# Causal attention scores on halves of the TensorE array, with the tokens of even sequences stored second half first

## What is computed

```
h      = x @ W.T + b + 2 * lora(x)                          # per sequence
q, k, v = dequant(h, 4-bit weights)                          # 32 query heads, 8 key/value heads, 128 wide
q, k   = rope(q), rope(k)                                    # tables by the token's place in its sequence
scores = q @ k.T / sqrt(128); scores = where(key <= query, scores, -max)
x      = x + dequant(softmax(scores) @ v, output weights)
x      = x + ffn(low_rank(x))                                # layer norm, two int8-like linears, gelu
```

## Time and profile before

| what | value |
|---|---|
| time, median of 3 runs (lowest to highest) | 568.68 us (568.56 to 568.96) |
| the profiled execution's own time | 569.7 us |
| its span, first to last instruction | 567.9 us |
| PE busy | 542.2 us, 95% |
| DVE busy | 485.0 us, 85% |
| POOL busy | 400.2 us, 70% |
| ACT busy | 363.0 us, 64% |
| granted TensorE clock, mean | 1.000 |

### The profile page before, as it was taken

How to read it: one execution, slowest core, us unless ns; L and a number is a source line. 1 busy time by engine, 2 the same in 40 slices (tenths; PEclk the granted TensorE clock), 3 DMA queues, 4 the chain that set the end, 5 groups by cost and what they waited for, 6 DMA issues and landing times.

```text
span 567.9 us, 10485 instructions
## 1 busy us (share of the span) xinstructions
PE 542.2 (95%) x3135; PEld 425.0 (75%) x3139; DVE 485.0 (85%) x626; ACT 363.0 (64%) x940; POOL 400.2 (70%) x410
## 2 busy tenths in 40 slices
PE   6999989999999999999999999999999999987885
PEld 3555768888888888888888888888888888865432
DVE  3553859997999799979997999799979998976897
ACT  3573567657665766576657665766576656665895
POOL 3005577799779977997799779977997799851063
PEclk9999999999999999999999999999999999999999
DMA  8752435422442244124512451245124312200003
GB/s 289 180 123 76 123 88 160 113 56 58 137 124 51 62 133 126 43 65 133 128 37 66 134 132 33 61 136 136 34 61 135 97 34 61 80 1 1 1 20 129
DMA packets 38172, 51.93 MB, mean 91 GB/s; under 512 B 12100, under 2 KB 20452, under 8 KB 38148
## 3 DMA queue, kind: packets, MB, share of 16 engines
q1 hardware_dynamic: 35652, 46.94, 31.3%
q10 hardware_dynamic: 2016, 3.48, 1.9%
q0 software_dynamic: 480, 1.22, 0.7%
HBM read 28.55 MB, written 2.10 MB: 54 GB/s over the span
## 4 chain that ended last, share of the span: by engine, by line
PE 80%; DVE 10%; issue 3%; DMA 2%; ACT 2%; POOL 2%; ACTq 0%; SPq 0%; DVEq 0%; POOLq 0%
PE pair L1378 23%; PE pair L1379 23%; PE flow L1367 9%; PE flow L1494 9%; PE flow L1486 4%; PE pair L1315 4%; DVE y_max L1191 2%; DVE raw_v L1081 1%; PE flow L1372 1%; DMA stage<-in_x 1%; PE flow L1315 1%; DMA swap_q<-raw_q 1%; DVE rope_c L1203 1%; DVE ctx_lo L1102 1%; DVE probs L1203 1%
## 5 line engine op out<-in xcount | busy, mean ns | idle before, releaser
L1095 DVE SCALAR_TENSOR_TENSOR accT<-pair,so_now,accT 128x1024 f32<-128x1024 f32 x125 | 157.2, 1274 | 14.8 <-PE pair L1379 13.9
L1081 DVE SCALAR_TENSOR_TENSOR raw_q<-pair,sc_now,raw_q 128x1024 f32<-128x1024 f32 x90 | 115.4, 1283 | 6.2 <-ACT raw_q L777 2.8
L560 POOL TENSOR_TENSOR probs<-probs,rowinv 128x512 f32<-128x512 f32 x64 | 66.8, 1044 | 65.4 <-DVE rowinv L1068 65.4
L722 ACT ACTIVATE probs<-flow,negmax 128x128 f32<-128x128 f32 x248 | 87.6, 369 | 32.8 <-DVE negmax L1049 32.8
L1378 PE MATMUL pair<-ctx_hi,wo 128*128 128x512 f32 x256 | 104.9, 410 | 2.8 <-issue 1.5
L1378 PE MATMUL pair<-h_hi,wq 128*128 128x512 f32 x240 | 100.0, 417 | 0.3 <-ACT raw_q L777 0.3
L1379 PE MATMUL pair<-ctx_lo,wo 128*128 128x512 f32 x256 | 100.2, 392 | 0.0
L1379 PE MATMUL pair<-h_lo,wq 128*128 128x512 f32 x240 | 94.1, 392 | 0.0
L529 POOL TENSOR_TENSOR rope_s<-swap_q,consts 128x512 f32<-128x512 f32 x62 | 80.2, 1293 | 9.2 <-DMA swap_q<-raw_q 9.2
L541 POOL TENSOR_TENSOR qT<-rope_c,rope_s 128x512 f32<-128x512 f32 x62 | 79.3, 1280 | 4.4
L529 POOL TENSOR_TENSOR rope_c<-raw_q,consts 128x512 f32<-128x512 f32 x62 | 78.8, 1293 | 0.0
(11 more groups left out here) (242 smaller groups left out, 966.3 us busy)
## 6 DMA issues: line engine op xcount, KB each, us to landing
swap_q<-raw_q SPq DMA_DIRECT2D x62, 256.0 KB, 3.7
wq_i<-in_L_attn_qw_q SPq DMA_DIRECT2D x8, 1024.0 KB, 5.6
wo_i<-in_L_attn_qw_o SPq DMA_DIRECT2D x32, 256.0 KB, 2.6
swap_k<-raw_k SPq DMA_DIRECT2D x14, 256.0 KB, 3.6
wkv_i<-in_L_attn_qw_k SPq DMA_DIRECT2D x8, 256.0 KB, 3.7
wkv_i<-in_L_attn_qw_v SPq DMA_DIRECT2D x8, 256.0 KB, 4.0
stage<-in_x ACTq DMA_DIRECT2D x4, 256.0 KB, 5.7
probs<-in_L_ffn_w ACTq DMA_DIRECT2D x4, 256.0 KB, 8.2
```

Source lines behind the costliest of these rows:

```text
L560: pool.tensor_tensor(pr, pr, rowinv[:, f, :].unsqueeze(2).broadcast_to([P, HB, P]), ALU.mult).then_inc(probs_done, 1)
L722: e = act.activation(probs[:, 0, f, seq(b)], bank[:, seq(b)], ACT.Exp, bias=negmax[:, f, b:b + 1], accum_out=rowsum[:, f, b:b + 1])
L1081: dve.scalar_tensor_tensor(out=into, in0=flat(pair[pair_of(h, (kind, j), last)][:, :, :]), scalar=sc_now[:, scale_slot(kind, h), j:j + 1], ...
L1095: dve.scalar_tensor_tensor(out=a, in0=flat(pair[pair_of(h, (O, c), last)][:, :, :]), scalar=so_now[:, (h if c == 0 else h - 1) % 2, c:c + ...
```

## The change

Tokens of sequences 0, 2, 4 and 6 are stored with tokens 64 to 127 first. Tables for cosine, sine and mask are made for a pair of sequences (even, odd) and are twice as wide, which makes the second constant DMA 907 columns instead of 523. x of an even sequence is loaded, and its output stored, by two DMAs of 64 rows each. Element counts of the POOL and ACT operations that read the tables stay; only their shapes are by pairs.

In `scores` each sequence becomes two products, each with 64 columns of queries as weights: the late 64 queries with all 128 keys, and the early 64 queries with the early 64 keys. The quarter that is wholly masked isn't computed and keeps the mask's value. Since late queries of an even sequence lie on partitions 0 to 63 and those of an odd one on 64 to 127, the two late products of a pair write different halves of the array's columns, and so do the two early ones. Line numbers behind `scores` move by 32.

```diff
-        tri = consts[:, K_TRI:K_TRI + P]
-        cos, sin = consts[:, K_COS:K_COS + P], consts[:, K_SIN:K_SIN + P]
+        tri = consts[:, K_TRI:K_TRI + 2 * P]
+        cos, sin = consts[:, K_COS:K_COS + 2 * P], consts[:, K_SIN:K_SIN + 2 * P]
...
+        HALVES = [slice(0, P // 2), slice(P // 2, P)]
+        def halves_of(b):
+            return HALVES if b % 2 else HALVES[::-1]
+        def load_x(eng, b):
+            if b % 2:
+                eng.dma_start(x_nat[b], x[b, :, :]).then_inc(d_x[b], 16)
+            else:
+                for here, there in zip(HALVES, halves_of(b)):
+                    eng.dma_start(x_nat[b][here, :], x[b, there, :]).then_inc(d_x[b], 16)
...
-                sp.dma_start(out[LOW_ORDER[b], :, :], y_out[b]).then_inc(d_out[b % 2], 16)
+                seat = LOW_ORDER[b]
+                if seat % 2:
+                    sp.dma_start(out[seat, :, :], y_out[b]).then_inc(d_out[b % 2], 16)
+                else:
+                    for here, there in zip(HALVES, halves_of(seat)):
+                        sp.dma_start(out[seat, there, :], y_out[b][here, :]).then_inc(d_out[b % 2], 16)
...
-                pe.wait_ge(d_x[b], 16)
+                pe.wait_ge(d_x[b], 16 if b % 2 else 32)
...
                 if not masked:
-                    pe.matmul(bank, ident_b[:, :], on_each_seq(tri_b[:, :]), start=True, stop=False)
-                for b in range(HB):
-                    t = seq(HB * f + b)
-                    mm = pe.matmul(bank[:, seq(b)], qT[:, par, t], kT[:, t], start=False, stop=(b == HB - 1), skip_group_check=masked)
+                    pe.matmul(bank, ident_b[:, :], on_each_pair(tri_b[:, :]), start=True, stop=True)
+                def tile(b, late):
+                    rows, keys = halves_of(b)[late], slice(0, P) if late else halves_of(b)[0]
+                    t = HB * f + b
+                    return pe.matmul(bank[rows, seq(b)][:, keys], qT[:, par, seq(t)][:, rows], kT[:, seq(t)][:, keys],
+                                     start=False, stop=True, skip_group_check=True)
+                for b in range(0, HB, 2):
+                    tile(b, 1)
+                    tile(b + 1, 1)
+                    tile(b + 1, 0)
+                    mm = tile(b, 0)
                 mm.then_inc(scores_done, 1)
```

More of the change, by code:

```diff
@@ L34 @@
 TINY = 1e-8
-K_ID, K_COS, K_SIN, K_TRI, K_ONE, K_BLK = 0, P, 2 * P, 3 * P, 4 * P, 5 * P
+K_ID, K_COS, K_SIN, K_TRI, K_ONE, K_BLK = 0, P, 3 * P, 5 * P, 7 * P, 8 * P
 K_MAG, K_PAR, K_END = K_BLK + B, K_BLK + B + 1, K_BLK + B + 3
@@ L46, in shape_constants @@
     inv = (np.float32(1.0) / np.power(np.float32(10000.0), np.arange(0, P, 2, dtype=np.float32) / np.float32(P)))
[L47 to L50, removed]
+    for j, place in enumerate((np.roll(np.arange(P), P // 2), np.arange(P))):
+        ang = (place.astype(np.float32)[None, :] * inv.astype(np.float32)[:, None]).astype(np.float32)
+        t[:, K_COS + j * P:K_COS + (j + 1) * P] = np.concatenate([np.cos(ang), np.cos(ang)], 0)
+        t[:, K_SIN + j * P:K_SIN + (j + 1) * P] = np.concatenate([-np.sin(ang), np.sin(ang)], 0)
+        t[:, K_TRI + j * P:K_TRI + (j + 1) * P] = np.where(place[:, None] >= place[None, :], 0.0, MASKED)
     t[:, K_ONE:K_ONE + P] = 1.0
@@ L80, in build @@
         ident_h = sb("ident_h", [P, P], F16)
-        tri_b = sb("tri_b", [P, P], BF16)
+        tri_b = sb("tri_b", [P, 2 * P], BF16)
         lora_parity = sb("lora_parity", [P, 2])
@@ L360, in per_seq, with per_pair, on_each_pair @@
             return ap.rearrange("p (b n) -> p b n", b=HB)
-        def on_each_seq(table):
-            return table.unsqueeze(1).broadcast_to([P, HB, P])
+        def per_pair(ap):
+            return ap.rearrange("p (b n) -> p b n", n=2 * P)
+        def on_each_pair(table):
+            return table.unsqueeze(1).broadcast_to([P, HB // 2, 2 * P])
+        HALVES = [slice(0, P // 2), slice(P // 2, P)]
[7 more added lines that the diff above has]
+                    eng.dma_start(x_nat[b][here, :], x[b, there, :]).then_inc(d_x[b], 16)
         block = ctx.enter_context(nc.Block())
@@ L462, in _ @@
                     sp.wait_ge(out_late, b - LATE_OUT + 1)
-                sp.dma_start(out[LOW_ORDER[b], :, :], y_out[b]).then_inc(d_out[b % 2], 16)
+                seat = LOW_ORDER[b]
[4 more added lines that the diff above has]
+                        sp.dma_start(out[seat, there, :], y_out[b][here, :]).then_inc(d_out[b % 2], 16)
             for s in d_out:
-                sp.wait_ge(s, 16 * (B // 2))
+                sp.wait_ge(s, 16 * (B // 2 + B // 4))
         @block.gpsimd
@@ L471, in _ @@
             for b in range(HB, B):
-                pool.dma_start(x_nat[b], x[b, :, :]).then_inc(d_x[b], 16)
+                load_x(pool, b)
             pool.dma_start(sc_nat[:, 0:P], sc_q.rearrange("g (h n) -> (g h) n", n=P)).then_inc(d_sc, 16)
@@ L489, in early_part @@
             def early_part(table, source, into, f, done):
-                pool.tensor_tensor(per_seq(into[:, f, :]), per_seq(source), on_each_seq(table), ALU.mult).then_inc(done, 1)
+                pool.tensor_tensor(per_pair(into[:, f, :]), per_pair(source), on_each_pair(table), ALU.mult).then_inc(done, 1)
             def early_add(count, f, target, parts, done):
@@ L528, in q_part @@
                         wait(pool, q_roped, 2 * n + f + 1)
-                        pool.tensor_tensor(per_seq(into[:, f, :]), per_seq(source[:, f, :]), on_each_seq(table), ALU.mult).then_inc(done, 1)
+                        pool.tensor_tensor(per_pair(into[:, f, :]), per_pair(source[:, f, :]), on_each_pair(table), ALU.mult).then_inc(done, 1)
                     def q_cosine(f):
@@ L544, in k_cosine @@
                         pool.wait_ge(swapped_k, 32 * g + 32)
-                        pool.tensor_tensor(per_seq(raw_k[:, f, :]), per_seq(raw_k[:, f, :]), on_each_seq(cos), ALU.mult).then_inc(k_cos, 1)
+                        pool.tensor_tensor(per_pair(raw_k[:, f, :]), per_pair(raw_k[:, f, :]), on_each_pair(cos), ALU.mult).then_inc(k_cos, 1)
                     def k_sine(f):
                         pool.wait_ge(swapped_k, 32 * g + 32)
-                        pool.tensor_tensor(per_seq(swap_k[:, f, :]), per_seq(swap_k[:, f, :]), on_each_seq(sin), ALU.mult).then_inc(k_sin, 1)
+                        pool.tensor_tensor(per_pair(swap_k[:, f, :]), per_pair(swap_k[:, f, :]), on_each_pair(sin), ALU.mult).then_inc(k_sin, 1)
                     def k_add(f):
@@ L633, in _ @@
             for b in range(HB):
-                act.dma_start(x_nat[b], x[b, :, :]).then_inc(d_x[b], 16)
+                load_x(act, b)
             act.dma_start(consts[:, P:K_END], const_dram[:, P:K_END]).then_inc(d_tables, 16)
@@ L794, in seed_mask @@
                         act.wait_ge(ctx_split, 2 * n + f + 1)
-                        act.activation(per_seq(flow[f][:, :]), on_each_seq(tri), ACT.Copy).then_inc(mask_seeded, 1)
+                        act.activation(per_pair(flow[f][:, :]), on_each_pair(tri), ACT.Copy).then_inc(mask_seeded, 1)
                     def keep_upper_context(f):
@@ L1000, in _ @@
             dve.tensor_scalar(lora_parity[:, :], parity, 2.0, None, ALU.mult).then_inc(mask_made, 1)
-            dve.tensor_copy(tri_b[:, :], consts[:, K_TRI:K_TRI + P]).then_inc(consts_made, 1)
+            dve.tensor_copy(tri_b[:, :], tri).then_inc(consts_made, 1)
             dve.wait_ge(mask_made, 1)
```

## The result

| | before | changed kernel |
|---|---|---|
| median (lowest to highest) | 568.76 us (568.56 to 568.96) | 579.5 us (579.16 to 580.01) |
| ratio, 95% interval | | 1.019 (1.0172 to 1.0207) |
| the profiled execution, its span | 569.7, 567.9 us | 579.16, 577.1 us |
| PE busy | 542.2 us | 550.5 us |

1.9% slower: 10.7 us by the medians, 9.2 us by the spans of the two profiled executions. The forecast was 576.0 us with a range of 571 to 583.

The account below looks back on a forecast made before the run. PE was taken to bound the kernel. Calls 53 x 0.12 + 7 x 0.07 plus 0.5 made +6.9 us, the start +0.4: +7.3, so 576.0 us from a median of 568.68, range 571 to 583.

Parts of the forecast that it names:

- What bounds the kernel: Loop: PE busy 56.72 of 57.0 us a period, so a microsecond PE loses costs one.
- Rounds: Score products: halves run two at a time, eight rounds a call, 0.67 us against 0.89, alone saving 0.22.
- rival: one after the other: Score calls: halves run singly, 1.34 us of rounds, 47 us more in all, 616 us; chance 3%.
- The pause: Each change of tile size around a call: some 0.09 us plus the weight load that used to be hidden.
- +0.12 us a call: Score calls: +0.14 going in, -0.02 inside and out; +0.07 where transposes follow; 6.9 us in all.
- The start, +0.4 us with bounds 0 and 1.7: Kernel start: extra DMA issues and a larger table delay x little, as bytes matter more than issue order.
- The prediction's own sign of being wrong: Pause particular to quarters, or something else on PE paid in the start beyond 1.7 us.
- The end and the wide table: Kernel end: last four outputs are whole, 0; table 197 KB larger, priced at nothing, 0.7 us if uncovered.
- The faster rival: Score calls: halves need no pause, each call saves 0.22 us, 13.2 in all, 555.9 us; chance 12%.

Follow-up runs that it names:

- half-pairs experiment: Changed kernel with the first pair of sequences of a call in halves, the second pair as whole products: 586.16 us, ratio 1.0291.
- split-loads run: Kernel before with only x of even sequences loaded by two DMAs of 64 rows each, in the old order: 573.35 us, ratio 1.0067.
- first joined placement: Both calls of a head side by side, first one moved behind a projection step; that order alone, whole products, on the kernel before: 570.73 us, 1.0019.
- control with both calls early: Kernel before, whole products, both calls of a head side by side at the first one's place, ahead of the projection step: 574.09 us, 1.009.

## Why the prediction was right, and what was off

**What bounds the kernel**: right, nearly one for one. Added up from the projection matmul ahead of each call to the second matmul behind it, the eight calls of a period are 0.96 us longer, and the period is 0.86 longer. PE takes 0.1 back where it waited for DVE: PEld's waits for DVE's draining of the PSUM pair (7 times, 1.9 us, in the row shown for the kernel before) have no counterpart with the change. The prediction, which read only PE's own waits, had left these out. It also expected PE's busy time to grow by less than the period, since pauses are idle; over the whole it did (8.3 of the span's 9.2 us), but in the two stretches, 1.00 us apart in width, it grew by 1.04, since the records of matmuls reach over the pauses.

**Rounds**: right. Each call's sixteen matmuls run two at a time, with starts 7 ns apart; 1.48 us a call would be about 2.15 had they run singly (rival: one after the other). 64-column halves behave as the quarters of the LoRA product do. The half-pairs experiment prices a pair's saving at 0.10 us against 0.11 predicted.

**The pause**: right, and it decides. The load for 64 columns takes 137 ns, where the prediction's 0.85 ns a column gives 136. Going in, the load starts 0.32 us after the last projection matmul, as predicted to 0.01; coming out, 0.07 before the end. This is shown by undoing it both ways: the same pauses with half of the products in halves lose another 1.0%, and one entry and one exit for two calls cost nothing against whole products in the same order. The Trainium skill ("TensorEngine Tiling (Array Packing)", Key Properties) has the array drained at a change of tiling mode and not at a change of tile; the trace agrees: at each change of size the next load starts 0.07 us before the recorded end of the last matmul, and between the halves there is no such pause.

**+0.12 us a call**: right. Measured 0.13 at the call shown, and 0.08 where transposes follow in the loop, predicted 0.07. Over the 60 calls the steps around them add up to +6.9 us, the sum that was predicted for them. Yet only 5.9 us lie between the two landmarks. The 1.0 is PE's waiting that the longer calls took in: some 0.7 in the six periods of the loop, the rest in the first and the last group.

**The start, +0.4 us with bounds 0 and 1.7**: the step that failed. It measured 3.2 us by the landmark, 3.8 us (0.67%) in the split-loads run. The prediction argued that the order of issue matters less than the bytes. But x1, with the same bytes, was issued 0.83 us later and landed 2.44 later (6.52 to 8.96); in seven executions with whole loads it landed at 5.4 to 6.9, in the five with split ones and the same gate at 8.9 to 9.6. The prediction also gave sequence 7 1.0 us of slack against two issues of 0.54, and left out that POOL issues nothing before x1 has landed: x7 was issued 3.5 us later and landed 3.8 later (16.18 to 19.99). Moving that gate to x0 gave back only some 0.8 us, so it is a part of the loss and not the larger one. And there was no term for PE itself, which idles 3.10 us ahead of x0 and then runs its transposes at half the pace. The forecast in spans was +7.3 and they show +9.2: 2.8 too little in the start, 1.0 too much in the calls.

The prediction's own sign of being wrong, more than 1.7 us in the start, came true, and x3 landed at 11.2 instead of 10.0 to 11.0. The time stayed within the range since the range was wide for the calls, where the forecast was good, and since PE's waits took 1.0 us in; as far as the start goes, that was luck.

**The end and the wide table**, priced at nothing: right; 0.2 us behind the loop, and 0.9995 for the table.

**The faster rival** (halves need no pause): refuted by the rows at 260.47 and 261.29.

Open: why x1's DMA takes 6.5 us instead of 4.9 behind two DMAs of 64 rows (in the trace SP's DMAs of W land sooner, after 4.0 and 6.1 us in the median instead of 4.6 and 7.3, which may be at its cost; that was not tested by itself), and which engine makes the order of the first joined placement 0.2% slower.

## What to carry to other kernels

Price a finer tile of the array by how often the kernel goes in and out of it, not by its products: here an estimated 0.22 us of products saved (twice the 0.11 of a pair) stood against some 0.34 us for one entry and one exit (0.22 and the 0.12 that a call lost). Two calls side by side turn the sum in the trace, but no version with halves came out faster than the kernel before. Look for the pause in the trace before writing the change: here each of the places where the tile size already changed showed it. And when a load is split in two, follow each semaphore that waits for its landing, on every engine, since a DMA issued behind such a wait takes its delay along.

## What was not expected of the hardware

The issue of a 64-row DMA on ACT's queue took 0.47 to 0.68 us (median 0.62), and the whole ones behind them 0.60, where whole ones had taken 0.45 to 0.50 before; in the first 10 us of the kernel the DMA engines moved 212 GB/s instead of 268, though they were busy for more of the time (windows, last two columns; the change first):

```profile
0.00:10.00 10.00, 5.67 (x19) 3.30 (x20) 0.50 (x2) 2.68 (x4) 0.95 (x6) 1.00 0.83 212
```

```profile
0.00:10.00 10.00, 6.28 (x30) 3.27 (x30) 1.88 (x4) 3.19 (x6) 3.39 (x10) 1.00 0.78 268
```

Part of this difference is that before, POOL had issued four more DMAs by then; from 4 to 6 us, ahead of these, it is 246 against 332 GB/s.

The granted clock in these rows is 1.00, 2.4 GHz. Yet after PE had been idle for 3.10 us, four fp32 transposes took 1.09 us instead of 0.60 to 0.66, up to some 12 us, as at 1.2 GHz; with matmuls in that idle time they took 0.60. That the idle time did it is not shown: the control with both calls early idled 0.36 us ahead of x0, and its first transposes took 1.08 us too, up to some 7 us. In the first microseconds of these spans the clock has to be read from the matmuls' own durations.
